# Second expert weights behind the first on each partition: two transfers for a pair of experts instead of four

## The reference, cut to what matters

```python
gu_e = x @ w13_e.T                       # 60 experts, w13_e is 352 x 256
h = silu(gu_e[:, :176]) * gu_e[:, 176:]
acc = acc + cw_e[:, None] * (h @ w2_e.T) # w2_e is 256 x 176
```

## Time and profile before

| what | value |
|---|---|
| median of three timed runs | 532.41 us |
| the profiled execution, its own time | 533.53 us |
| its span in the trace | 531.7 us |
| mean granted TensorE clock | 0.946 |
| attention | about 38 to 280 us |
| shared expert and router | about 280 to 318 us |
| experts, in pairs | about 318 to 500 us |
| last scatters, loading of `ychoice`, sum | 500 to 531.7 us |

### The profile page before, as it was taken

How to read it: one execution, slowest core, us unless ns; L and a number is a source line. 1 busy time by engine, 2 the same in 40 slices (tenths; PEclk the granted TensorE clock), 3 DMA queues, 4 the chain that set the end, 5 groups by cost and what they waited for, 6 DMA issues and landing times.

```text
span 531.7 us, 7870 instructions
## 1 busy us (share of the span) xinstructions
PE 471.9 (89%) x2752; PEld 250.8 (47%) x2752; DVE 342.6 (64%) x739; ACT 219.9 (41%) x321; POOL 212.9 (40%) x227
## 2 busy tenths in 40 slices
PE   7989999999999999986599999888988888897892
PEld 4544333333333332354467766555655555564561
DVE  7478799999999996047889455344333443443447
ACT  2477578878788788941214111001010000010032
POOL 2077202022020220004304536666666566674516
PEclk8898799999999999998889999899889898998997
DMA  8970000000000000001100003666867576773164
GB/s 281 338 207 1 0 2 1 1 2 1 0 1 2 1 2 0 2 0 39 41 1 1 16 20 121 202 222 201 248 213 219 176 233 212 220 250 121 36 254 149
DMA packets 33617, 53.68 MB, mean 101 GB/s; under 512 B 6870, under 2 KB 21918, under 8 KB 33584
## 3 DMA queue, kind: packets, MB, share of 16 engines
q1 hardware_dynamic: 27728, 44.82, 26.7%
q0 software_dynamic: 5856, 8.43, 5.2%
HBM read 50.71 MB, written 10.09 MB: 114 GB/s over the span
## 4 chain that ended last, share of the span: by engine, by line
PE 66%; DVE 17%; issue 5%; another core or an unknown queue 4%; DMA 2%; POOL 2%; ACT 2%; SPq 1%; POOLq 0%; DVEq 0%; ACTq 0%
PE EP L1475 14%; PE PV L1285 12%; PE M L1239 8%; PE EP L1272 5%; PE EP L1275 5%; PE EP L1469 3%; DVE mx L838 2%; PE PV L1498 2%; PE PV L1492 2%; PE EP L1376 2%; PE M L1492 2%; DMA w<-ychoice 2%; DVE xh L770 2%; PE M L1297 1%
## 5 line engine op out<-in xcount | busy, mean ns | idle before, releaser
L838 DVE TENSOR_REDUCE mx<-M 128x1 f32<-128x512 f32 x256 | 159.3, 683 | 14.7 <-PE M L1239 14.5
L667 ACT ACTIVATE QS<-EP 128x1024 f32<-128x1024 f32 x128 | 123.9, 1021 | 26.7 <-PE EP L1275 26.3
L1475 PE MATMUL EP<-w,QS 128*128 128x352 f32 x244 | 92.5, 505 | 11.6 <-DVE QS L1049 9.2
L719 ACT ACTIVATE QS<-EP 128x176 f32<-128x176 f32 x61 | 19.4, 318 | 166.8 <-PE EP L1475 93.1
L490 POOL DMA_INDIRECT QS<-h2rows,tab x61 | 63.3, 1037 | 52.4 <-issue 16.7
L1049 DVE COPY QS<-EP 128x256 f32<-128x256 f32 x61 | 25.8, 424 | 90.4 <-PE EP L1469 55.1
L495 POOL DMA_INDIRECT ychoice<-QS,tab x61 | 61.9, 1015 | 28.4 <-issue 26.0
L1285 PE MATMUL PV<-QS,VA 128*32 128x512 f32 x512 | 69.1, 612 | 0.0
L1475 PEld LDWEIGHTS EP<-w,QS 128*128 128x128 f32 x244 | 45.7, 201 | 41.8 <-issue 16.2
L1239 PE MATMUL M<-KT,QT 64*128 64x512 bf16 x256 | 59.6, 395 | 2.3 <-DVE mx L838 1.9
L1272 PE MATMUL EP<-QT,KT 64*128 64x512 bf16 x256 | 49.8, 381 | 0.4 <-ACT QS L667 0.2
(11 more groups left out here) (255 smaller groups left out, 641.2 us busy)
## 6 DMA issues: line engine op xcount, KB each, us to landing
w<-in_w SPq DMA_DIRECT2D x30, 704.0 KB
w<-in_w SPq DMA_DIRECT2D x61, 112.0 KB
w<-ychoice SPq DMA_DIRECT2D x8, 512.0 KB, 7.8
w<-in_w SPq DMA_DIRECT2D x30, 128.0 KB
segu<-in_segu SPq DMA_DIRECT2D x1, 1408.0 KB, 10.5
x<-in_x SPq DMA_DIRECT2D x2, 512.0 KB, 5.0
wide<-in_wmod SPq DMA_DIRECT2D x1, 1024.0 KB, 8.0
h2rows<-xh SPq DMA_DIRECT2D x2, 512.0 KB, 2.9
```

Of the source, the lines that this page charges most:

```text
L667: nc.scalar.activation(PT[n % 3][:, 2 * p:2 * p + 2, :], EP[p][:, :, :], ACT.Exp, scale=HD ** -0.5).then_inc(e_done, 1)
L838: nc.vector.tensor_reduce(out=mx[:, u % 2, q, j, c:c + 1], in_=src, axis=AX.X, op=ALU.max).then_inc(m_free, 1)
L1475: ins = mm(BANK[b][:, 0:I13], XGT[b][:, c * P:(c + 1) * P], w13[:, r, c * I13:(c + 1) * I13], start=c == 0, stop=c == NC - 1)
```

## The change

The row of second weights of each partition is laid behind the first weights in DRAM and in the ring. `w13` becomes 960 numbers wide on each partition: 704 of first weights, and 256 of the expert's own second weights on partitions 0 to 111 (zeros on the other 16). One transfer with rows of 3840 bytes brings both; a second brings the 128 shared rows. For an odd expert the host now takes hidden rows 64 to 175 as its own and rows 0 to 63 as shared, as the row order of `w2_in` had it before. The overflow expert still needs three transfers, from a third array with the plain order. `YG` lies wholly in the widened ring. The memory used on each partition is the same: 28160 + 15360 bytes before, 38400 + 5120 after.

```diff
-        w13 = sb("w13", [P, RING, NC * I13])
-        w2 = sb("w2", [P, RING // 2, 3, D])
+        w13 = sb("w13", [P, RING, W1])
+        w2 = sb("w2", [P, RING // 2, D])
...
-        w2f = w2[:, :, :, :].rearrange("p r i n -> p (r i n)")
-        YG = [v[:, TOPK * D * b:TOPK * D * (b + 1)].rearrange("p (k n) -> p k n", k=TOPK)
-              for v, b in [(ringf, b) for b in range(NT - 2)] + [(w2f, 0), (w2f, 1)]]
+        YG = [ringf[:, TOPK * D * t:TOPK * D * (t + 1)].rearrange("p (k n) -> p k n", k=TOPK) for t in range(NT)]
...
                 sp.dma_start(w13[:, k:k + 2, :], w13_in[bass.ds(e, 2), :, :].rearrange("e p n -> p e n")).then_inc(ld_w[k // 2], 16)
-                sp.dma_start(w2[0:OWN, k // 2, 0, :], w2_in[bass.ds(e * I, OWN), :]).then_inc(ld_w[k // 2], 16)
-                sp.dma_start(w2[:, k // 2, 2, :], w2_in[bass.ds(e * I + OWN, 2 * SHARED), :]).then_inc(ld_w[k // 2], 16)
-                sp.dma_start(w2[0:OWN, k // 2, 1, :], w2_in[bass.ds(e * I + OWN + 2 * SHARED, OWN), :]).then_inc(ld_w[k // 2], 16)
+                sp.dma_start(w2[:, k // 2, :], w2_in[bass.ds(e * SHARED, 2 * SHARED), :]).then_inc(ld_w[k // 2], 16)
...
-                    mm(BANK[6 + i][:, 0:D], HST[b][0:OWN, (1 + i) * P:(2 + i) * P], w2[0:OWN, s, i, :], start=True, stop=False)
+                    mm(BANK[6 + i][:, 0:D], HST[b][0:OWN, (1 + i) * P:(2 + i) * P], w13[0:OWN, 2 * s + i, W1 - D:W1], start=True, stop=False)
...
-                    mm(BANK[6 + i][:, 0:D], HST[b][half, 0:P], w2[half, s, 2, :], start=False, stop=True).then_inc(m_y, 1)
+                    mm(BANK[6 + i][:, 0:D], HST[b][half, 0:P], w2[half, s, :], start=False, stop=True).then_inc(m_y, 1)
...
-                pair(q, 2 * q, 2 * q, 64, lambda i: 16 * ((2 * q + i) // BUFS + 1), q)
+                pair(q, 2 * q, 2 * q, 32, lambda i: 16 * ((2 * q + i) // BUFS + 1), q)
...
+    behind = np.zeros((E, P, D), np.float32)
+    behind[0::2, 0:own] = w2[0::2, 0:own]
+    behind[1::2, 0:own] = w2[1::2, shared:I]
+    rest = w2[:, own:I].copy()
+    rest[1::2] = w2[1::2, 0:shared]
+    arrays["w13"] = np.concatenate([w13, behind], axis=2)
+    arrays["w2"] = rest.reshape(E * shared, D)
+    arrays["w2any"] = w2.reshape(E * I, D)
```

More of the change, by code:

```diff
@@ L13, in adaln_layer @@
 def adaln_layer(nc, x_in, cos_in, sin_in, c_in, wmod_in, wqkv_in, wo_in, wr_in, segu_in, sedn_in,
-                w13_in, w2_in, h2rows, ychoice, out):
+                w13_in, w2_in, w2any_in, h2rows, ychoice, out):
     f32, bf16, i32, u32 = mybir.dt.float32, mybir.dt.bfloat16, mybir.dt.int32, mybir.dt.uint32
@@ L35, in adaln_layer @@
     NE, TOPK = 60, 4
-    I13 = w13_in.shape[2] // NC
+    W1 = w13_in.shape[2]
+    I13 = (W1 - D) // NC
     I = I13 // 2
@@ L318, in overflow_weights @@
                 x = sp.value_load(ovei[0:1, bass.ds(b, 1)], min_val=0, max_val=NE - 1)
-                sp.dma_start(w13[:, 0, :], w13_in[bass.ds(x, 1), :, :].rearrange("e p n -> p (e n)")).then_inc(done, 16)
-                sp.dma_start(w2[0:OWN, 0, 0, :], w2_in[bass.ds(x * I, OWN), :]).then_inc(done, 16)
-                sp.dma_start(w2[0:SHARED, 0, 2, :], w2_in[bass.ds(x * I + OWN, SHARED), :]).then_inc(done, 16)
+                sp.dma_start(w13[:, 0, 0:W1 - D], w13_in[bass.ds(x, 1), :, 0:W1 - D].rearrange("e p n -> p (e n)")).then_inc(done, 16)
+                sp.dma_start(w13[0:OWN, 0, W1 - D:W1], w2any_in[bass.ds(x * I, OWN), :]).then_inc(done, 16)
+                sp.dma_start(w2[0:SHARED, 0, :], w2any_in[bass.ds(x * I + OWN, SHARED), :]).then_inc(done, 16)
             for k in range(4, RING):
@@ L1524, in _ @@
             for q in range(RING // 2):
-                pair(q, 2 * q, 2 * q, 64, lambda i: 16 * ((2 * q + i) // BUFS + 1), q)
+                pair(q, 2 * q, 2 * q, 32, lambda i: 16 * ((2 * q + i) // BUFS + 1), q)
             with pe.Fori(0, (LAPS - 2) // 2) as o:
                 for k in range(RING, 3 * RING, 2):
-                    pair(o * RING + k // 2, o * (2 * RING) + k, k, o * 128 + 64 * (k // RING + 1),
+                    pair(o * RING + k // 2, o * (2 * RING) + k, k, o * 64 + 32 * (k // RING + 1),
                          lambda i: o * (2 * RING // BUFS * 16) + 16 * ((k + i) // BUFS + 1))
             for e in range(NE - RING, NE, 2):
-                pair(e // 2, e, e, 64 * LAPS, lambda i: 16 * ((e + i) // BUFS + 1))
-            pe.wait_ge(ld_w[0], 64 * LAPS + 48)
+                pair(e // 2, e, e, 32 * LAPS, lambda i: 16 * ((e + i) // BUFS + 1))
+            pe.wait_ge(ld_w[0], 32 * LAPS + 48)
             gate_up(NE + 1, 0, 0)
@@ L1591 @@
         "sedn": a["ffn_se_down_w"].T,
-        "w13": a["ffn_w13"].reshape(E, I2, NC, P).transpose(0, 3, 2, 1).reshape(E, P, NC * I2),
-        "w2": a["ffn_w2"].transpose(0, 2, 1).reshape(E * I, D),
-    }
+    }
+    own, shared = 112, I - 112
+    w13 = a["ffn_w13"].reshape(E, I2, NC, P).transpose(0, 3, 2, 1).reshape(E, P, NC * I2)
+    w2 = a["ffn_w2"].transpose(0, 2, 1)
+    behind = np.zeros((E, P, D), np.float32)
[6 more added lines that the diff above has]
+    arrays["w2any"] = w2.reshape(E * I, D)
     arrays = {k: np.ascontiguousarray(v) for k, v in arrays.items()}
```

## The result

The changed kernel took 533.28 us (median of 20 runs, 527.36 to 538.92). The kernel before took 535.46 us (median of 20 runs, 531.11 to 538.73, the three runs shown above among them), 3 us more than the median of those three. The ratio is 0.9941 with a 95% interval of 0.9913 to 0.9968: 0.6% faster, where 527.5 us had been forecast, 0.9% less than 532.41 and 1.5% less than 535.46. This ratio leaves out three of the changed kernel's 20 runs as slow and none of the kernel before, which flatters the change; the medians of all 20 give 533.28 / 535.46 = 0.9959. Two later comparisons of the same kernel gave 0.9967 (0.9931 to 1.0002) and 0.9981 (0.9951 to 1.0010). Weighted by their intervals the three make 0.996 (0.994 to 0.998). The kernel is faster by about 0.4%, some 2 us; of the three intervals only the first excludes 1.

What follows compares the result with a forecast made beforehand. The prediction took PE's work at 4.82 us a pair plus 32.6 us of stops to bound the experts' stage. Fewer packets were to save 5 us, all other terms 0: 533.5 to 528.5 us profiled, 527.5 us median, range 514 to 538 us.

Steps and rivals of the forecast that it cites:

- the frame: Only the experts' stage can gain: 24 pairs at 6.18 us, 4.82 us without stops; attention is untouched.
- stops: Time in the experts' stage beyond 4.82 us a pair, 32.6 us over 24 pairs, read as PE's signals coming late.
- Weights are early: In the experts' stage, weights arrive some 9 us before use, so no wait of PE is for them.
- the line through 1024 and 5632 bytes: DMA engine time of a weight packet: 7 ns plus 38 ns per 1000 bytes, giving 153 ns for 3840 bytes.
- the long rows load badly: Rival: 3840-byte weight rows load slowly, about 60 engine-us a pair, and stops grow to 537 or 544 us; chance 0.21.
- something that the transfers load also carries the signals: Experts' stage: PE's finished-work signals come about 2 us late because DMA transfers load what carries them.
- packets and completions, by 30%: 9.8 us. I take 5 us: Stops in the experts' stage shrink 9.8 us if they follow packets and completions, 0.3 us if engine time; 5 us taken.
- waits called remote: Sign in the experts' stage: DVE's waits that no event in the trace explains become fewer and shorter at L1049.
- the address instruction: Sign: SP's instruction of L300 in the experts' stage, once stretched from 46 to 702 ns, stays near 46 ns.
- packets don't matter: Sign of a wrong forecast: the same distance between pair loads in the experts' stage with 30% fewer packets.
- nothing changes: Rival: the experts' stage's stops follow bytes or engine time, or not transfers at all; 529.7 to 535 us, chance 0.29.
- The stops all but vanish, and POOL becomes the bound: Rival: experts' stage falls to POOL's 5.32 us a pair, 20.6 us less, 512 us; chance 0.11.

Runs made afterwards that it cites:

- e9: Changed kernel with the experts' results stored by SP's plain transfers to fixed rows instead of POOL's indirect ones (results wrong): 496.69 us, ratio 0.9358 to the kernel before.
- e6: Changed kernel loading only 64 bytes of each shared second-weight row in the loop (results wrong), where the stops are: 530.44 us, ratio 0.9984 to the kernel before.
- e12: The same kernel as e6 with more rounds: 528.93 us, ratio 0.9983 to the kernel before.
- e1: Changed kernel loading only 64 bytes of each shared second-weight row in the loop (results wrong), on chip 1: 501.72 us, ratio 0.9934 to the kernel before.
- e4: Changed kernel loading only the first half of each 3840-byte row in the loop (results wrong), on chip 1: 504.42 us, ratio 0.9976 to the kernel before.
- e3: Changed kernel with the wide transfer of a pair split into one for each expert, on chip 1: 506.92 us, ratio 1.0011 to the kernel before.
- the first group: Runs on chip 1: e1, e3, e4 and the changed kernel with rows cut in five; the kernel before took 505.28 us there, and no trace had a stop.
- group 4: A later set of runs on a chip of its own, where the stops are; the kernel before took 531.28 us, the changed kernel 529.34 us.
- e11: Changed kernel with rows gathered by SP's plain transfers from fixed rows, scatters left to POOL (results wrong): 501.21 us, ratio 0.941 to the kernel before.
- e13: Kernel before the change with results stored by SP's plain transfers to fixed rows (results wrong): 497.82 us, ratio 0.9333 to the unedited kernel before.
- e14: The same kernel as e9 with more rounds: 495.67 us, ratio 0.9300 to the kernel before.
- e10: Changed kernel with both gathers and scatters replaced by SP's plain transfers at fixed rows (results wrong): 499.26 us, ratio 0.9406 to the kernel before.
- e15: Changed kernel with results of two experts in five stored by SP to a side table, POOL doing the rest (results wrong): 515.84 us, ratio 0.963 to the kernel before.

## Why the prediction was right or wrong

**Right: the frame.** Attention is unchanged. The experts' stage runs at 4.82 us a pair plus stops of some 30 us, and e9 shows it: without stops and with fewer transfers on POOL, 24 pairs go at 4.84 us. Weights are early: no wait of PE names them in any run, with five times the rows, half the bytes or one transfer more. What the prediction put down to stops alone, 32.6 us, was in part the lower clock behind them. The Trainium skill's fixed 2 us for a DMA ("DMA: Bandwidth & Descriptors", anatomy of one DMA, where it is fitted to transfers that POOL issues, and SP issues these) does not show. By it two exposed transfers would have been an estimated 4 us a pair, and the traces have 6.16 after 6.18 us a pair.

**Right: what the change does to the queue.** 599 packets a pair were forecast at about 600. Engine time was worked out as 1% less and came out 4% less (54.1 after 56.5 engine-us), so rows of 3840 bytes load no worse than the line through 1024 and 5632 bytes says, and the rival "the long rows load badly" (60 engine-us) is out.

**Wrong: the step "something that the transfers load also carries the signals", and with it "packets and completions, by 30%: 9.8 us. I take 5 us".** The distance between loads stayed at 6.16 us where about 6.0 was named as right; waits called remote were to become fewer and did not; the address instruction was to stay near 46 ns and reached 711. The first is what the prediction had listed as "packets don't matter". e6 and e12 then took nearly all load of the weights away and kept the stops, at ratios of 0.9984 and 0.9983: instead of 5 us, the whole load of the weights is worth about 1 us, and 3 at most by the intervals. The stops follow POOL's indirect transfers (0.93 to 0.94 without half of them). The range of 514 to 538 us holds the 533.28 us, but in the case "nothing changes" (529.7 to 535), so this is no merit of the mechanism. SP's stretched address instruction, which had pulled me toward the packets, is a mark of the stops and not of the load: in e9, at 0.98 of DMA between its first and 25th issue, the longest took 52 ns. What had misled me was one comparison, attention against the experts' stage: both the weights' loads and POOL's indirect transfers are absent from the first and present in the second. The trace of before had held a hint against the loads: by DVE's remote waits the stops come 9 to 21 us apart, while pairs are loaded every 6.2 us in the mean.

**The rivals.** "The stops all but vanish, and POOL becomes the bound" is not what the change does, but it is a state that exists: e1 to e4 ran in it, at 5.1 to 5.2 us a pair instead of the 5.32 that I had worked out from POOL's two transfers, since POOL starts the loop ahead: in e3 it issued 94 transfers, two for each of 47 experts, in the 125.1 us in which PE did 48. "Nothing changes" is nearly it: its reason (the stops have nothing to do with the weights' transfers) is what the runs support.

**Where the 0.4% comes from is open.** Hardly any load at all gives 0.9984 and 0.9983 where the stops are, with intervals that reach 1, so the changed transfers cannot be worth much more than that through traffic; in the first group it gives 0.9934. In group 4 the changed kernel (0.9981) and the one with hardly any load (0.9983) gained alike, and 0.9981 lies where the expectation had put "nothing is left that could gain". Without stops, the kernel before with SP's stores is at 0.9333 and the changed one at 0.9300, a difference smaller than either interval. The three direct comparisons all lie below 1, and no experiment places the gain.

**How POOL's transfers delay PE's signals is open too.** Shown is that the stops go when the gathers or the scatters are issued by SP, and that they don't follow the weights or the rows in a gather. That a queue or a memory that these transfers use also carries the signals is only argued. It is not even shown that the signals are late: the ends of matmuls in these traces are modelled, so PE's work itself may have ended 2 us late, and no run tells the two apart. SP's address instruction, which waits for nothing of PE and was stretched as well, speaks against it without excluding it. Nor does any run say why POOL's transfers bring no stops on chip 1. SP's versions also change the addresses (fixed rows instead of scattered ones), and no version that puts every row in its place with fewer indirect transfers was tried.

## What to carry to other kernels

Before you price a wait by the traffic beside it, list everything that the waiting stretch has and the quiet one lacks, and take each away alone: here one run with almost no weight loads, beside a kernel before that has the stops, would have moved the forecast from 5 us to about 1. Look at the granted clock behind a wait too: the wait may be only part of its price. Fewer and longer transfers are worth next to nothing where they are hidden, here two fewer a pair and 30% fewer packets for 0.4%. The gain to look for in this kernel is in POOL's queue: half its indirect transfers fewer is worth 6 to 7% where the stops are, if it can be had with every row in its place.

## What the runs showed of the hardware that was not expected

- With two indirect transfers an expert on POOL (1.02 us each, and 0.31 us before the next), finished work of PE is at times noticed 2 us late by ACT, DVE, SP and POOL together. It was so in the first comparison and in groups 2 to 4, and not on chip 1 (e1 to e4). With one an expert (e9, e11, e13, e14) or none (e10) no such wait was seen, at a DMA share of 0.85 to 0.92 from 320 to 460 us.
- Within one stop, works of PE that ended one after another can be noticed about 1.4 us apart. In the kernel before, DVE's remote waits end at 368.57 and 370.00 us:

```profile
368.57 0.29 DVE L1041 COPY QS<-M 128x128 f32<-128x128 f32 x1 [1.00 <-remote]
370.00 0.42 DVE L1060 TENSOR_TENSOR QS<-PV,MOD 128x256 f32<-128x256 f32 x1 [0.57 <-remote]
```

- The kernel before takes 505 us in one group and 531 to 536 us in the others; the traces of the first (e1 to e4) have no stops. The granted clock of the loop differs as well: 1.00 from 320 to 460 us in e1 and e3, 0.94 to 0.95 from 325 to 465 us in e6 and e12. In the changed kernel it was 0.50 from 381 to 384 us, after PE had stood still until 379.95. It was 1.00 over the loop of e15, in spite of the stops there.
- A gather of 64 rows costs POOL 949 ns, one of 128 rows 1024 ns: half the rows save 7%.
